# Cross attention's turned outputs and projection copied out of the step bank by ScalarE, VectorE works from the copies

## The reference

```python
a1 = softmax(logits_1); a2 = softmax(logits_2)      # 16 heads, (112, 375) each
lam = exp(lambda_q1 @ lambda_k1) - exp(lambda_q2 @ lambda_k2) + 0.2
attn_output = einsum('bhts,bhsd->bhtd', a1 - lam * a2, v) * (1.0 - 0.2)
output = attn_output.reshape(B, T, D) @ out_proj_weight.T + out_proj_bias
x = layernorm(x + output)
```

## Time and profile before

| | us |
|---|---|
| median of 3 runs | 1797.75 |
| lowest, highest | 1795.05, 1801.78 |
| the profiled execution | 1796.06 |
| its span | 1794.3 |
| TensorE busy in the span | 1566.2 |
| VectorE busy | 1128.1 |
| ScalarE busy | 900.5 |
| GpSimd busy | 757.1 |

### The profile page before, as it was taken

How to read it: one execution, slowest core, us unless ns; L and a number is a source line. 1 busy time by engine, 2 the same in 40 slices (tenths; PEclk the granted TensorE clock), 3 DMA queues, 4 the chain that set the end, 5 groups by cost and what they waited for, 6 DMA issues and landing times. The chain is left out here.

```text
span 1794.3 us, 46494 instructions
## 1 busy us (share of the span) xinstructions
PE 1566.2 (87%) x17664; PEld 1195.9 (67%) x17664; DVE 1128.1 (63%) x2617; ACT 900.5 (50%) x2175; POOL 757.1 (42%) x920
## 2 busy tenths in 40 slices
PE   4899999984999999999999999829999999999991
PEld 2677777763566666666666666518898898898891
DVE  4566666662888788778888888634444444444443
ACT  2344455442466666666666666604444443443444
POOL 6334444322755556765676567421121111121112
PEclk9999999997799999999999999959999999999996
DMA  6666776634455545554554455167776766766744
GB/s 178 180 188 187 194 195 186 193 113 99 136 139 142 149 138 136 164 153 136 141 161 145 134 154 153 49 224 250 245 267 215 245 228 228 246 216 229 260 143 173
DMA packets 205508, 318.92 MB, mean 178 GB/s; under 512 B 61000, under 2 KB 174056, under 8 KB 205288
## 3 DMA queue, kind: packets, MB, share of 16 engines
q1 hardware_dynamic: 183784, 249.78, 45.3%
q0 software_dynamic: 21504, 66.19, 12.6%
HBM read 224.52 MB, written 91.03 MB: 176 GB/s over the span
## 5 line engine op out<-in xcount | busy, mean ns | idle before, releaser
L1154 DVE TENSOR_REDUCE cross_mx<-cross_bank_max 112x2 f32<-112x750 f32 x512 | 460.2, 931 | 115.4 <-PE cross_bank_max L1273 113.1
L985 ACT ACTIVATE cross_probs<-cross_bank_score 125x448 f32<-125x448 f32 x768 | 406.2, 545 | 238.2 <-PE cross_bank_score L1263 235.4
L1461 POOL DMA_INDIRECT acc<-experts_y,experts_dest_i x64 | 100.0, 1562 | 459.4 <-DMA acc<-experts_y,experts_dest_i 260.6
L1263 PE MATMUL cross_bank_score<-cqst,ckst 97*125 97x448 f16 x768 | 282.7, 370 | 4.7 <-ACT cross_probs L985 2.4
L1273 PE MATMUL cross_bank_max<-ckst,cqst 96*112 96x375 f16 x1024 | 257.5, 334 | 28.8 <-DVE cross_mx L1154 21.1
L1538 DVE TENSOR_TENSOR experts_hid<-experts_bank_h,experts_gated 128x256 f32<-128x256 f32 (+1 forms) x288 | 113.4, 394 | 245.2 <-ACT experts_gated L1487 240.2
L1572 PE MATMUL experts_bank_h<-experts_x_hi,w 128*128 128x256 f16 (+1 forms) x1536 | 239.1, 267 | 22.3 <-DVE experts_hid L1538 20.9
L1289 PE MATMUL cross_bank_out<-cross_probs,cross_val 125*32 125x112 f32 x6144 | 201.6, 264 | 0.1
L1572 PE MATMUL experts_bank_h<-experts_x_lo,w 128*128 128x256 f16 (+1 forms) x768 | 198.9, 267 | 0.0
L1273 PEld LDWEIGHTS cross_bank_max<-ckst,cqst 96*112 96x112 f16 x1024 | 128.9, 133 | 89.1 <-DVE cross_mx L1154 36.3
L1487 ACT ACTIVATE experts_gated<-experts_bank_h 128x256 f32<-128x256 f32 (+1 forms) x288 | 103.1, 358 | 155.2 <-PE experts_bank_h L1572 152.5
(11 more groups left out here) (245 smaller groups left out, 3045.1 us busy)
## 6 DMA issues: line engine op xcount, KB each, us to landing
w<-w_halves SPq DMA_DIRECT2D x24, 3072.0 KB, 11.8
experts_w_third<-w_halves SPq DMA_DIRECT2D x12, 3072.0 KB, 11.7
cross_ew<-in_experts POOLq DMA_DIRECT2D x32, 768.0 KB, 5.6
w_halves<-cross_ew_half POOLq DMA_DIRECT2D x32, 768.0 KB
ckst<-cross_k SPq DMA_DIRECT2D x96, 187.5 KB
cross_v<-front_v SPq DMA_DIRECT2D x24, 531.2 KB
cross_val<-cross_v SPq DMA_DIRECT2D x32, 398.4 KB
front_src<-in_ctx_t SPq DMA_DIRECT2D x24, 500.0 KB, 6.0
```

The source lines that it names most:

```text
L985: nc.scalar.activation(probs[:, e % PROBS], bank_score[e % 2][0:SC, 0:4 * T], ACT.Exp, scale=CROSS_SCALE).then_inc(probs_ready, 1)
L1154: nc.vector.tensor_reduce(mx[:, b % nb, 2 * n:2 * n + 2], bank_max[n % 2][0:T, :, 0:S], AX.X, ALU.max).then_inc(max_read, 1)
L1263: nc.tensor.matmul(bank_score[e % 2][0:SC, 0:pair_w], kst[:, p, g, k * SC:(k + 1) * SC], qst[:, p, g, :], start=True, stop=True).then_inc( ...
```

## The change

ScalarE gets three more readings of the step bank per pass, `out1` in part 8, `proj` in part 14 and `out0` in part 19, each behind that part's exponential: plain copies into new SBUF tiles `sums` (112 x 512, one for each half) and `projected` (112 x 256, one for each of three batches). They give the bank free. VectorE's reciprocal, product and `r` read these tiles, wait for the copies (`read[name]`), and signal two new semaphores, `prod_ready` and `r_ready`, for which the copies into the same tile wait, one batch later for `sums` and three for `projected`. GpSimd's bias add waits for `r_ready`. The weights buffer `w` shrinks from two slots to one, and the experts stage holds the other two in `w_more`.

```diff
@@ cross, tiles and semaphores
+        sums = ph.sb("sums", [T, 2, 512], F32)
+        projected = ph.sb("projected", [T, nb, D], F32)
+        prod_ready, r_ready = ph.sem("prod_ready"), ph.sem("r_ready")
@@ cross, sync
-                        sp.dma_start(w[:, 0].rearrange("p q h n -> p q (h n)"),
+                        sp.dma_start(w.rearrange("p q h n -> p q (h n)"),
@@ cross, gpsimd
-                        wait(pool, read["proj"], c - nb + 1)
+                        wait(pool, r_ready, c - nb + 1)
@@ cross, scalar: step_read
+                    elif name in ("out0", "out1"):
+                        h = int(name[-1])
+                        wait(act, prod_ready, 2 * b + h - 1)
+                        nc.scalar.activation(sums[:, h], bank[0:T, :], ACT.Copy).then_inc(read[name], 1)
+                    elif name == "proj":
+                        wait(act, r_ready, b - nb + 1)
+                        nc.scalar.activation(projected[:, p], bank[0:T, 0:D], ACT.Copy).then_inc(read[name], 1)
@@ cross, scalar: loop
-                        for name in ("row1", "heads", "row0", "turn", "score"):
+                        for name in ("row1", "out1", "heads", "proj", "row0", "out0", "turn", "score"):
@@ cross, vector: normalise
-                    unit = bank[0:T, :].rearrange("p (u w) -> p u w", w=32)
-                    wait(dve, full[name], b + 1)
+                    unit = sums[:, h].rearrange("p (u w) -> p u w", w=32)
+                    wait(dve, read[name], b + 1)
@@
-                                            ALU.mult).then_inc(read[name], 1)
-                    wait(dve, read[name], b + 1)
+                                            ALU.mult).then_inc(prod_ready, 1)
+                    wait(dve, prod_ready, 2 * b + h + 1)
@@ cross, vector: loop
-                            wait(dve, full["proj"], b + 1)
+                            wait(dve, read["proj"], b + 1)
@@
-                            nc.vector.tensor_tensor(r[:, p], bank[0:T, 0:D], x_bias[:, p], ALU.add).then_inc(read["proj"], 1)
-                            wait(dve, read["proj"], b + 1)
+                            nc.vector.tensor_tensor(r[:, p], projected[:, p], x_bias[:, p], ALU.add).then_inc(r_ready, 1)
+                            wait(dve, r_ready, b + 1)
@@ experts
-        w_third = ph.sb("w_third", [128, CUTS, 2, CUT], F16)
+        w_more = ph.sb("w_more", [128, 2, CUTS, 2, CUT], F16)
-        w_slot = lambda j: w_third if j % 3 == 2 else w[:, j % 3]
+        w_slot = lambda j: w_more[:, j % 3 - 1] if j % 3 else w
@@ decoder
-        w = ctx.enter_context(nc.sbuf_tensor("w", [128, 2, CUTS, 2, CUT], F16))
+        w = ctx.enter_context(nc.sbuf_tensor("w", [128, CUTS, 2, CUT], F16))
```

## The result

| | before | changed |
|---|---|---|
| median, us (10 runs each, one chip) | 1798.11 | 1805.62 |
| lowest, highest | 1795.05, 1802.02 | 1804.44, 1818.12 |
| span of the profiled execution | 1794.3 | 1802.7 |

The ratio is 1.0055, 95% interval 1.0036 to 1.0074: slower by about half a per cent, 7.5 us between the medians. The forecast of 1800 was 5.6 us low, and the time lies inside the range. "No change that can be told", within 0.5%, was the likeliest case there; the measured ratio lies on its edge.

What follows compares the result with a forecast made beforehand. TensorE, 87% busy, sets the pace, with VectorE's chain a second limit close behind. 30 x (0.11 - 0.07) = +1.2, collisions +1.1, tail +1.0 make +3.3 us: 1800 forecast, range 1790 to 1811.

Steps and rivals of the forecast that it cites:

- The projection's copy: Part 14, ScalarE: copy takes 0.38 us, row0's wait falls from 0.85 to 0.51, VectorE's `r` starts 0.12 later.
- the lead: TensorE starts row0's transpose 0.34 us earlier per batch; forecast to be gone at the next part's first maxima.
- out0's wait: Part 19: VectorE, free at 502.37 or earlier, idles for ScalarE's copy until 502.55 before its reciprocal, +0.18 us.
- The reciprocal: VectorE at out0 and out1: 0.18 us out of SBUF against 0.25 out of PSUM, gaining 0.07 each.
- The CAST: GpSimd operation blocking VectorE's sum into `heads`; both slip alike, so next part's first maxima, max(0), come 0.12 us later.
- the sum escaping: Rival: VectorE's sum into `heads` starts before GpSimd's CAST in twelve batches, -3.7 us, 1796; chance 0.10.
- Collisions: VectorE products, now with two SBUF inputs, wait for GpSimd operations; three over all batches, +1.1 us.
- The tail: After batch 31 nothing covers the copies and hand-overs before the experts stage: +1.0 us.
- L914 blocks too: Rival: GpSimd's L914 holds VectorE's product as the CAST holds the sum, +7.4 us, 1807; chance 0.07.
- ScalarE is late: Rival: projection copy ends 0.34 us later, row0 gains nothing, out0's copy holds VectorE longer; 10.2 more, 1810; chance 0.10.
- The lead is kept: Rival: out0's copy does not hold up VectorE, row0's 0.34 us stays; 12.3 us faster, about 1784; chance 0.08.
- A gain can come from these three alone: Cross attention: TensorE's waits at L1307, L1273 and L1319, 42 us in 27 batches, are the only source of gain.

Runs made afterwards that it cites:

- kernel 6: The changed kernel run once more beside the kernel before: 1808.56 us, ratio 1.0057.
- kernel 8: The kernel before with only GpSimd's bias add moved behind its four small operations: 1805.89 us, ratio 1.0032.
- kernel 2: The kernel before with ScalarE's copy of the projection alone (weights buffer in its new place): 1872.58 us, ratio 1.004.
- kernel 3: The kernel before with ScalarE's copy of out0 alone (weights buffer in its new place): 1902.12 us, ratio 1.0196.
- kernel 9: The kernel before with the projection's copy, weights buffer in its new place, and GpSimd's bias add held until the batch's projection is done: 1795.38 us, ratio 0.9973.
- Kernel 1: The kernel before with only the weights buffer's new place: 1867.85 us, ratio 1.0009.
- kernels 1 to 4: The kernel before with the weights buffer's new place, alone or plus one copy (projection, out0, out1 in turn): ratios 1.0009, 1.004, 1.0196, 1.0004.

## Why the prediction was right, and where it was not

**The projection's copy** took 0.39 (0.38), row0's wait 0.51 (0.51), `r` 0.426 (0.41). Right in each number; and the lead was used up within the batch, as forecast.

**out0's wait** was put at 0.18 on the reciprocal. It was 0.26: counted from row0's start the reciprocal came at 4.16 us (544.90 - 540.74), before at 3.56 (502.37 - 498.81), 0.60 later, of which the lead of 0.34 goes off. The copy began 0.44 after its exponential, as reckoned. But that exponential came 3.10 after row0 where it had been 3.00: 0.09 of the lead was gone before this part. Some of it went at the maxima matmul of 542.65, which followed the end of a reduction by 0.05; the rest is spread over the matmuls between. The forecast had taken the lead as whole here. This is the first mis-sized term, +0.08.

**The reciprocal** is the step that failed: 0.248 for 0.18. The price had been taken from a reciprocal with half as many results, and source and size were mixed up in it; that 0.248 and 0.252 stand for 16 results out of SBUF, strided and side by side, and 0.171 for 8, shows that the size is what counts. So the gain of 0.07 is missing at both places. At out0 the net is +0.26 and not +0.11, and at out1 0 and not -0.07.

**The CAST** hid part of this. The forecast let CAST and sum slip alike; in fact the CAST began 0.28 after the product instead of 0.41, the sum was held less (0.58 for 0.70), and of the +0.26 only +0.14 came through to max(0). So a plain pass rose by 0.14 (8.89 to 9.03, the other half unchanged at 12.79), where +0.12 and -0.07 had been put down. With the reciprocal's gain at its lower bound of nothing, which the forecast kept in its range, the same sum would have given 30 x 0.18 = 5.4 instead of 1.2, and 1805 on the median. That this meets the measured 1805.6 is in part luck: the plain pass rose by 0.14 and not 0.18, the collisions were fewer, and the profiled execution has stretches at the lower clock that the sum knows nothing of.

The range had one end that its own sum does not give: the sum escaping and a full reciprocal gain come to 1796 less 0.6, not to 1790. Nothing hung on it.

**Collisions.** Put at three products and +1.1 us. There are two (1.33 and 0.87 us), and the group's busy time rose from 27.1 to 28.5. The shorter began at 1109.97, 0.12 behind GpSimd's L920, which issues a transfer, and ended 0.35 behind the start of the CAST after it. The longer, at the place of the earlier trace rows:

```profile
974.49 1.33 DVE L1049 TENSOR_TENSOR cross_prod<-cross_sums,cross_weight 112x256 f32<-112x256 f32 x1
```

```profile
974.38 1.16 POOL L923 TENSOR_TENSOR cross_ew_half<-cross_ew_big,cross_ew_half 128x512 f16<-128x512 f32 x1
```

**The tail** took 41.87 us from the last score matmul to the first of `experts`, before 40.81: +1.06 for +1.0 (kernel 6: 41.74).

**The signs named beforehand.** Come true: L1307's wait at 0.5 and owed to the copy, VectorE idle before out0's reciprocal and released by ScalarE. Near: ScalarE 39 us busier and not 48, since the records overlap. Not: the reciprocal at 0.18; max(0)'s wait over 0.6, which stayed at 0.22 while a second one of 0.21 appeared at the maxima just before it (547.34 below); and a pass of at most 21.7.

```profile
547.34 0.53 PE L1283 MATMUL cross_bank_max<-ckst,cqst 96*112 96x375 f16 x2 [0.21 <-DVE cross_mx L1164]
...
548.28 0.50 PE L1283 MATMUL cross_bank_max<-ckst,cqst 96*112 96x375 f16 x2 [0.22 <-DVE cross_mx L1164]
```

**The rival "L914 blocks too"** fell: at 545.19 and 545.40 the weight product (two SBUF inputs) took 0.17 and the product 0.42 with L917 (L914 of before) still running until 545.61. The Trainium skill (SBUF — State Buffer, Who interferes with whom) would have both blocked; the trace does not agree for these two, and does for the CAST, L923 and the bias add. For L914 it agrees in part: a step that begins in its first 0.46 us is held to the end of them, as in kernel 8 above, and in the kernel before at 480.15, where GpSimd had been idle for 5.3 us ahead of L914:

```profile
480.15 0.54 DVE L1034 TENSOR_TENSOR cross_weight<-cross_recip,cross_coef 112x16 f32<-112x16 f32 x1
```

```profile
480.05 1.49 POOL L914 TENSOR_SCALAR cross_ew_big<-cross_ew 128x512 f32<-128x512 f32 x1 [5.31 <-DMA w_halves<-cross_ew_half]
```

The forecast's rows all had L914 well under way, so the rival falls where it was priced. In the changed kernel seven weight products of passes with scattered rows begin in this stretch and lose 0.05 to 0.13 each, about 0.8 us that no term of the sum holds.

**"ScalarE is late"** fell too: row0 gained its 0.34, and out0's copy was 0.09 late and not 0.34. **"The lead is kept"** was given one condition, that out0's copy did not hold up VectorE. Without that copy the lead does reach part 0, together with the sum's escape, which the forecast priced as another rival (0.34 and 0.31; measured 0.65 in kernel 2). It is then spent at two places that no row of the forecast shows, ScalarE's copy of the turned rows (0.35) and the bias add's collision (0.41). "A gain can come from these three alone" was right as the waits stood; it left out the wait that appears once one of them shrinks.

**Not foreseen: TensorE's granted clock.** It has two levels, 2.4 and 1.2 GHz, and falls to the lower one in short stretches. Windows of the changed kernel (length, then busy time of PE, PEld, DVE, ACT, POOL with counts, granted clock, DMA share, GB/s), and one of the kernel before at the same place of the same pass:

```profile
1010.00:1032.00 22.00, 20.01 (x269) 13.06 (x269) 20.32 (x51) 15.72 (x37) 12.84 (x17) 1.00 0.48 138
1032.00:1044.00 12.00, 11.34 (x149) 7.79 (x150) 8.49 (x18) 6.73 (x16) 8.36 (x9) 0.86 0.48 141
```

```profile
1030.00:1042.00 12.00, 11.08 (x154) 7.40 (x152) 9.89 (x21) 7.41 (x18) 8.26 (x9) 1.00 0.52 123
```

TensorE worked for 20.0 of the 22 us before the clock fell; the window of before has it as full (11.1 of 12) with no fall. Pass 26 took 24.10 with the fall in it, pass 18, with the same work, 22.61. Behind its first pass the stage of the kernel before has 3.4 us at the lower level, that of the changed kernel 10.2, the same kernel's other profiled execution 23.9, kernel 3 102, kernel 9 3.4. So these stretches differ between executions of one kernel, and are far more where batches stall. The changed kernel has 3.4 us of them more in pass 26 and 3.4 more in pass 29; at the 1.5 us of pass 26 they make, as an estimate, 3 of the stage's 6.0 us. How much of the 7.5 us between the medians is theirs is open. **Nor the landing** of row0's transfer: in several passes with scattered rows the next batch's first score matmul waited 0.1 to 1.2 us (before the change 0.3 to 0.8, in three of them) and followed the landing by 0.09, so there VectorE's chain was not the limit that the forecast took it for. The ten passes with scattered rows took 21.82 in the mean, before 21.70.

## What to carry to other kernels

Moving a read from one engine to another is priced by what the first engine then waits for: the exponential and the copy ahead of it were longer than the read that they replaced, and the same instruction cost the same out of either memory. Take the price of an instruction from a row with the same number of results, not only the same source. And before a lead is counted, follow it around the whole batch past every operation of another engine that could hold the one that comes earlier: the projection's copy brought 0.65 us in one half of the pass and lost it all in the other, to two steps that were in nobody's waits before, GpSimd's bias add and ScalarE's copy of the turned rows; with the bias add out of the way 0.30 stayed. The parts of a change do not add up either: two that cost +0.10 and +2.7 alone cost +0.14 together.

## What the runs showed of the hardware

- A VectorE reciprocal of 112 x 16 takes 0.247 us out of the bank, 0.248 out of SBUF with a stride, 0.252 side by side; products of 112 x 256 take 0.42 from either memory.
- A VectorE step with two SBUF inputs that begins during GpSimd's CAST or tensor_tensor ends late by what the other has left, less 0.14: 0.36 late behind 0.50 of CAST in kernel 3, 0.91 behind 1.05 of L923 in the changed kernel. It works the other way too: L923 that began with a product at 798.73 took 1.43 and not 1.16.
- Behind the start of GpSimd's TENSOR_SCALAR (128 x 512, 1.49 us) such a step is held only to 0.46 us after it: 0.36 late when it began 0.10 after (kernel before, 480.15), 0.20 at 0.25 (kernel 8), and so in all 54 cases in the traces of this case. Of the 490 that began later in it, 488 ran free (0.01 late at most).
- A ScalarE copy of 512 columns out of a bank takes 0.59 us written in order, and 1.03 written with a stride of 16 elements.
- The kernel before takes 1798 to 1802 us in some sets of runs and 1866 to 1869 in others. Kernel 1, which differs in the buffer's place alone, has plain passes equal to its own to 0.01 us at the higher total, and 56 of the 68 us between the two spans lie in passes 10 to 14, 18 to 22 and 26 to 30, around those in which GpSimd scatters rows. The record gives the number 11 to the chip of kernels 1 to 4 and 10 to that of all the later ones, with 1800 us in two sets and 1869 in the last; so whether the chip makes the difference, or something else that changed between sets, is not shown.
